# Row sums of a long attention on four 32-column tiles of the array, and their reciprocals one round later

## What is computed

```python
# b = 16 batches, s = 56 queries, h = 16 heads, l = 1500 keys, d = r = 64
q_r    = jnp.einsum('bshq,hqr->bhsr', q_big, W_qr)
k_r    = jnp.einsum('bld,hdr->bhlr', kv_rope, W_kr)
scores = jnp.einsum('bhsr,bhlr->bhsl', q_r, k_r)
attn   = jax.nn.softmax(scores, axis=-1)
ctx_c  = jnp.einsum('bhsl,bld->bhsd', attn, kv_rope)
ctx_lat = jnp.einsum('bhsd,hkd->bshk', ctx_c, w_kc_kv)
out = ctx_lat.reshape(b, s, H * K) @ Wo.T
```

## Time and profile before

| | us |
|---|---|
| median of 3 runs | 2405.49 |
| lowest, highest | 2403.42, 2409.81 |
| the profiled execution's own time | 2404.89 |
| its span, first to last instruction | 2403.1 |
| PE busy (share of the span) | 2208.8 (92%) |
| DVE busy | 1469.7 (61%) |
| POOL busy | 1125.4 (47%) |
| ACT busy | 958.9 (40%) |

### The profile page before, as it was taken

One profiled execution on the slowest core, in us unless ns is written; L12 is line 12 of the kernel. 1 busy time (PEld: TensorE's weight loads), 2 busy tenths in 40 slices (PEclk: granted clock), 3 DMA queues, 4 the chain that ended last, 5 costly groups with the idle time before them and its releaser, 6 DMA issues. The chain is left out here.

```text
span 2403.1 us, 37321 instructions
## 1 busy us (share of the span) xinstructions
PE 2208.8 (92%) x13148; PEld 1532.7 (64%) x13148; DVE 1469.7 (61%) x2468; ACT 958.9 (40%) x1433; POOL 1125.4 (47%) x612
## 2 busy tenths in 40 slices
PE   6768998989999998897999999899799999998998
PEld 4447997745555557664555555698365555567997
DVE  2765444277777756787777775412677777745444
ACT  1443443334445451212454445111345445533443
POOL 0331332037777770363777777011067777731332
PEclk9878998789999998997999999879799999998999
DMA  4473631365464513124545542286755544402332
GB/s 81 138 247 92 214 122 51 87 176 113 105 135 105 124 39 123 43 92 111 131 103 116 125 102 60 61 292 265 199 122 113 120 109 109 103 9 94 121 120 80
DMA packets 123792, 285.54 MB, mean 119 GB/s; under 512 B 33282, under 2 KB 76028, under 8 KB 119721
## 3 DMA queue, kind: packets, MB, share of 16 engines
q1 hardware_dynamic: 122984, 281.96, 44.0%
q0 software_dynamic: 672, 1.84, 0.2%
HBM read 237.15 MB, written 46.41 MB: 118 GB/s over the span
## 5 line engine op out<-in xcount | busy, mean ns | idle before, releaser
L1226 DVE TENSOR_REDUCE keep_top<-banks 128x1 f32<-128x500 f32 x945 | 603.2, 674 | 242.7 <-PE banks L1150 238.5
L1296 ACT ACTIVATE att_ex<-banks 125x896 f32<-125x896 f32 x576 | 524.5, 919 | 241.0 <-PE banks L1143 222.0
L1175 PE MATMUL banks<-att_ex,att_v 125*64 125x448 f32 x2304 | 464.8, 545 | 0.0
L1349 POOL TENSOR_TENSOR att_acc<-att_acc,att_ex 125x896 f32<-125x896 f32 x186 | 391.4, 2104 | 130.4 <-ACT att_ex L1296 116.8
L1150 PE MATMUL banks<-keep_kh,keep_qt 64*128 64x500 f32 x1008 | 364.6, 449 | 31.1 <-PEq L574 10.7
L1349 POOL TENSOR_TENSOR att_acc<-att_acc,att_two 125x896 f32<-125x896 f32 x141 | 296.6, 2103 | 118.0 <-DVE att_two L1238 118.0
L1175 PEld LDWEIGHTS banks<-att_ex,att_v 125*64 125x64 f32 x2304 | 152.5, 136 | 246.9 <-issue 182.9
L1143 PE MATMUL banks<-att_ql,keep_kh 64*125 64x448 f32 x1152 | 299.1, 366 | 0.0
L1143 PE MATMUL banks<-att_sh,att_on 64*125 64x448 f32 x1152 | 297.4, 365 | 0.0
L1664 PE MATMUL banks<-moe_xs,moe_w 128*128 128x448 f32 x1272 | 278.8, 369 | 5.3 <-DVE moe_w L1760 3.7
L1238 DVE TENSOR_TENSOR att_two<-att_ex 125x896 f32<-125x896 f32 x144 | 235.9, 1638 | 62.9 <-ACT att_ex L1296 56.8
(11 more groups left out here) (271 smaller groups left out, 2761.4 us busy)
## 6 DMA issues: line engine op xcount, KB each, us to landing
keep_kh<-kvt_hi SPq DMA_DIRECT2D x96, 375.0 KB, 5.1
att_kl<-kvt_lo SPq DMA_DIRECT2D x96, 375.0 KB, 7.1
q_rows<-mats_q SPq DMA_DIRECT2D x24, 896.0 KB, 4.4
keep_qt<-q_rows SPq DMA_DIRECT2D x96, 224.0 KB, 5.8
moe_raw<-L_experts_dram SPq DMA_DIRECT2D x53, 384.0 KB, 4.1
att_v<-kvn SPq DMA_DIRECT2D x24, 720.0 KB
sort_wu<-L_experts_dram SPq DMA_DIRECT2D x14, 1024.0 KB, 10.1
moe_cb<-comb_rows SPq DMA_DIRECT2D x62, 224.0 KB
```

What stands on the lines that cost most here:

```text
L1175: last = pe.matmul(PS[WEIGHED][64 * e:64 * e + 64, 0:HALF], v[:, s // 2, u, s % 2, :], ex[:, u % RING, e, :], start=u == 0, stop=u == UNIT ...
L1226: dve.tensor_reduce(top[:, s % 2, n // NS, n % NS:n % NS + 1], PS[6 + (PIECES * s + n) % 2][:, 0:SB], AX.X, ALU.max).then_inc(mx_done, 1)
L1296: act.activation(ex[:, u % RING], scored, ACT.Exp).then_inc(exp_done, 1)
L1349: pool.tensor_tensor(a, a if n else ex[:, 0], two[:, i] if k == 2 else ex[:, k], ALU.add).then_inc(gathered, 1)
```

## The change

Five things are done at once.

1. On PE the row sums of batch b-1 are made by `sums_by_quarters`: four matmuls of 32 columns of ones by 224 columns of `att_acc`, each into its own 32 partitions of the bank SUMMED. At a stage's end the three-part sum (`sums`) stays as it was.
2. `att_sm` has 224 columns instead of 448, and ACT copies as many.
3. SP writes the row sums to memory with one DMA from the partitions 0, 32, 64 and 96 instead of two DMAs. The semaphore's counts follow.
4. On SP `shifts(b+1)` now stands ahead of `scales(b-1)`, and on DVE `invert` stands in the third round, ahead of the pair sum, instead of in the second behind it.
5. On GpSimd `place(b-2)` stands in the first round of batch b behind the pair's gather, where `place(b-1)` stood in the last round.

```diff
-        cu, rsb, sm = st.sb("cu", [128, 2, HALF]), st.sb("rsb", [128, 2, HALF]), st.sb("sm", [128, HALF])
+        cu, rsb, sm = st.sb("cu", [128, 2, HALF]), st.sb("rsb", [128, 2, HALF]), st.sb("sm", [128, HALF // 2])
...
                     sp.wait_ge(sm_done, b + 1)
-                    for e in range(2):
-                        sp.dma_start(G["rs"][2 * b + e:2 * b + e + 1, :], sm[64 * e:64 * e + 1, :]).then_inc(sum_out, 16)
-                    sp.wait_ge(sum_out, 32 * b + 32)
+                    sp.dma_start(G["rs"][2 * b:2 * b + 2, :].rearrange("e (q n) -> (e q) n", q=2), sm[0:128:32, :]
+                                 ).then_inc(sum_out, 16)
+                    sp.wait_ge(sum_out, 16 * b + 16)
...
                         sums(b - 1)
-                        scales(b - 1)
                     if b < B - 1:
                         shifts(b + 1)
+                    if b:
+                        scales(b - 1)
...
+                def sums_by_quarters(total):
+
+                    for j in range(4):
+                        n = HALF // 2 * (j % 2)
+                        last = pe.matmul(PS[SUMMED][32 * j:32 * j + 32, 0:HALF // 2], one[:, 0:32],
+                                         total[:, j // 2, n:n + HALF // 2], start=True, stop=True)
+                    last.then_inc(sums_ready, 1)
...
-                            sums([acc[:, (s + 1) % 2]])
+                            sums_by_quarters(acc[:, (s + 1) % 2])
...
+                        if i == ROUNDS - 1 and not known(b, 1):
+                            invert(s + 1, b - 1)
                         if i == ROUNDS - 1 and not left:
                             last_pair(b)
                         pair(b, i)
-                        if i == 1 and not known(b, 1):
-                            invert(s + 1, b - 1)
...
-                        act.wait_ge(sum_out, 32 * b)
-                    act.activation(sm[:, :], PS[SUMMED][:, 0:HALF], ACT.Copy).then_inc(sm_done, 1)
+                        act.wait_ge(sum_out, 16 * b)
+                    act.activation(sm[:, :], PS[SUMMED][:, 0:HALF // 2], ACT.Copy).then_inc(sm_done, 1)
...
-                            if i == ROUNDS - 1 and k == 1 and b:
-                                place(b - 1)
+                            if i == 0 and k == 2 and b > 1:
+                                place(b - 2)
                 place(B - 2)
```

## The result

The changed kernel takes 2385.57 us (median of 4 runs, 2381.28 to 2389.64) against 2404.45 us for the kernel before in the same comparison. The ratio is 0.992, with a 95% interval from 0.9902 to 0.9939: 15 to 24 us faster. The forecast was 2386. The profiled execution took 2381.28 us, its span is 2379.5 us.

What follows compares the result with a forecast made beforehand. PE, busy 1023.66 of 1033.79 us in the long attention's stages, was taken as the bound. 2404.89 - 11.2 (row sums) - 8.4 (DVE's wait) = 2385.3, plus 0.6 for the median: forecast 2386, range 2380 to 2399.

Steps and rivals of the forecast that it cites:

- What bounds the kernel: Long attention's three stages: PE's queue sets the time, busy 1023.66 of 1033.79 us.
- Quarters side by side: PE's row sums: eight passes in two groups of four about 0.19 us apart, 0.37 us in all.
- three steps: Rival for PE's row sums: quarters overlap only partly, 0.69 us against 0.75, time 2394; chance 0.12.
- two at a time: Rival for PE's row sums: no more than two quarters overlap, time 2403, no measurable change; chance 0.08.
- one after the other: Rival for PE's row sums: quarter-width tiles don't overlap at all, 39 us more, time 2436.5; chance 0.04.
- factor of 3.07: PE's row sums: eight passes take 0.49 us, gain 0.13 a batch, 5.9 us, time 2391; no chance of its own.
- One more changeover: PE around the row sums: 32-column tiles add a changeover of 0.11 us, 0.13 with the weights.
- The term of 11.2 us: PE's row sums in quarters: 0.50 us instead of 0.75, 0.25 a batch over 45 batches.
- The term of 8.4 us: DVE's inversion one round later: removes eighteen waits for the row sums' DMA, 26.4 - 18 x 1.0.
- a room of 1.0 us: DVE's wait for the row sums: 1.0 us of each costs nothing, PE loses what is over it.
- What is moved with it: SP's DMAs and loads, DVE's inversion and GpSimd's placing in new places: cost 0 in all.
- The 6 us for placings at the stages' ends: GpSimd at the stages' ends: what one uncovered placing at each of three ends could cost; booked at 0.

Runs made afterwards that it cites:

- e5: The changed kernel with the four quarter matmuls of each batch issued twice, the second time over the first; 2404.01 us.
- e6: The changed kernel with two matmuls of 64 columns by 224 instead of four of 32, leaving out half of the row sums' columns (wrong results); ratio 0.9879.
- e2: The kernel before with only the moves (inversion in the third round, shifts ahead of scales, placing in the next batch), row sums in halves; 2396.96 us.
- e3: The kernel before with SP issuing the loads of the values behind the shifts instead of ahead of the row sums' transfers; 2394.1 us.
- e9: The kernel before with quartered row sums and the values' loads behind the shifts; inversion, scales and placing as before; 2385.19 us.
- e1: The kernel before with only the row sums in quarters; inversion, scales and placing where they stood; 2397.08 us.
- e4: The changed kernel with the scales ahead of the shifts on SP again; 2585.07 us.
- e10: The changed kernel with GpSimd's placing back in the last round, between the gathers; 2389.08 us.

## Why the prediction was right

- **What bounds the kernel.** Right for 27 of the 45 batches of the kernel before, and for all of the changed kernel: e5 adds two steps of 0.187 us to PE, and the batch grows by 0.383. The 18 others are taken up below.
- **Quarters side by side.** The likeliest case came: two groups of four, 0.21 us apart (0.19 forecast; the 0.02 are about what the first group's records are longer than the second's, 377 ns against 353, and the sum had 0.02 for the first weights). The rivals with three steps, two at a time or one after the other fall: two steps took 0.40 us. The estimate in the prediction from the Trainium skill's factor of 3.07 for four row tiles ("TensorE: Matmul & The Clock Gate", Part 3) gave 0.49, and four column tiles did better here.
- **One more changeover.** Right in kind and size: 0.10 us (0.11 from L1165), and 0.13 with the weights by e6. It was looked for on the wrong side: L1151 was to start 0.60 us after L1184 and starts 0.52 after it, because the new changeover lies ahead of L1184. The sum of both stretches, 0.99 us where 1.22 stood, comes out as forecast.
- **The term of 11.2 us.** Measured 11.1 us between e2 and the changed kernel, 10.6 between e3 and e9.
- **The term of 8.4 us.** Measured 7.7 in e2 and 8.1 in e3. The estimate by a room of 1.0 us was a little too high: in the shorter waits the room was 1.0 to 1.1 us, and one wait of 0.80 us cost nothing, where the sum counted it as a gain of 0.2 us.
- **What is moved with it.** Its cost of 0 held in the sum: no wait for att_rsb but three of 8.7 us in all (four of 9.3 before), no wait for keys or lows. The 6 us for placings at the stages' ends did not come: e9 has the placing in its old round and the same sum of batches.
- **What the prediction did not see.** It added the two parts as if each were worth its own sum. That held only because both were made, and nothing in the working looks at it: in this the prediction was lucky. Alone the quarters give 5.1 us and the order 7.7; the missing 6.0 us is the growth of DVE's 18 waits in e1. Had the change been the quarters alone, the same working would have forecast 11 us and been wrong by half. The step that it left out: in the 18 disturbed batches PE is not the bound, a DMA is, and what PE saves ahead of that wait is given back at it.
- **The sum** of the parts, 19.6 us, stands against 18.8 in the batches and 18.9 between the medians.

## What to carry to other kernels

Where matmuls fill a quarter of the array's columns and stand far from others of their tile, four of them side by side pay only what is left after one more change of the tile, about 0.13 us here; put users of the same tile next to each other. Before a saving on the busiest engine is multiplied by the number of rounds, take out the rounds whose pace is set by a transfer that was issued ahead of the saving: there the saving only lengthens the wait. And a tiny transfer that somebody waits for belongs ahead of the bulk loads on its queue, or its user so late that it does not matter; either cure gave the same time.

## What the runs showed that I had not expected

**The clock after a wait of PE.** In e4 PE stands three to five microseconds for att_sh in 39 batches, 130 us, but the kernel loses 199. Windows of 3 us around one such wait, busy times, then the granted clock (last but two):

```profile
678.00:681.00 3.00, 0.99 (x8) 0.54 (x8) 1.26 (x2) 0.55 (x1) 1.93 (x1) 1.00 0.34 77
681.00:684.00 3.00, 1.89 (x10) 1.72 (x12) 0.00 (x0) 0.92 (x1) 0.00 (x0) 0.66 0.60 145
684.00:687.00 3.00, 3.00 (x24) 2.44 (x21) 2.21 (x4) 1.58 (x2) 1.07 (x1) 0.77 0.99 216
687.00:690.00 3.00, 3.00 (x18) 1.06 (x16) 2.19 (x3) 1.15 (x2) 1.58 (x2) 1.00 1.05 230
```

PE's timeline across it, rows of L1143 ahead of the wait and behind it:

```profile
678.22 0.36 PE L1143 MATMUL banks<-keep_qt,keep_kh 64*125 64x448 f32 x2
678.42 0.37 PE L1143 MATMUL banks<-keep_qt,att_kl 64*125 64x448 f32 x2
...
682.11 0.74 PE L1143 MATMUL banks<-att_sh,att_on 64*125 64x448 f32 x2 [3.12 <-DMA att_sh<-keep_nmh]
682.64 0.58 PE L1143 MATMUL banks<-keep_qt,keep_kh 64*125 64x448 f32 x2
683.01 0.58 PE L1143 MATMUL banks<-keep_qt,att_kl 64*125 64x448 f32 x2
```

PE has stood for 3.12 us when L1143 starts at 682.11. Then the granted clock is down, and the pairs of L1143 follow at 0.37 us, which is the lower level of 1.2 GHz, instead of 0.20 at 2.4 GHz. Over the 45 batches of e4 the clock is 0.93 to 0.94 against 1.00 in the changed kernel. My expectation of 170 us had waits alone, and more of them than came; the 69 us over the measured 130 are not in it. As an estimate, 1260.38 us at 0.93 hold some 84 us less at full speed, part of it within the waits, so the clock can carry the 69. PE's stalls in the first stage of the kernel before, 0.82 us at the longest, left the clock at 1.00.

**The placing is longer beside DVE's pair sum.** It took 2.0 us in the kernel before, next to DVE's pair sum, and takes 1.16 us in its new place, where in 39 of 45 cases DVE is busy all or nearly all the time with row maxima (L1235). In e10 it stands in its old round again, but waits for the reciprocals until the pair sum is over, and takes 1.15. All placings, before, after and in e10 (ns, shortest, median, longest):

```profile
L1357 POOL TENSOR_TENSOR ctx_ctxT<-att_cu,att_rsb x45: 1419/1999/2013, 557.7 to 2131.8; 128x448 f32<-128x448 f32 x45
...
L1366 POOL TENSOR_TENSOR ctx_ctxT<-att_cu,att_rsb x45: 1147/1157/1787, 564.5 to 2109.8; 128x448 f32<-128x448 f32 x45
...
L1366 POOL TENSOR_TENSOR ctx_ctxT<-att_cu,att_rsb x45: 1141/1154/2060, 562.5 to 2119.1; 128x448 f32<-128x448 f32 x45
```

So it is the pair sum that counts, not the round and not a busy DVE as such. The pair sum in its turn takes 1.09 us in the 48 cases of the changed kernel in which GpSimd is idle, and about 1.98 where one of GpSimd's sums covers half of it, while these sums of 125x896 take 2.1 us in either case. In all the placings take 53.5 us instead of 88.4, more than the 32 us by which GpSimd is less busy, and the prediction's 2.0 us for one was too much. It cost and brought nothing here: e9, with the placing in its old round, has the same sum of batches.
